# One slot's filler exchanged: Bm's products behind the gate's in slot 4, two blocks of y in slot 6, and the gate evicted at the end of slot 4

## What is computed

```
for each of the 128 steps:
    r        = decay * r + ctx_t * ctx_t
    inp      = (norm(x)_t * r) @ Wi.T + bi
    gate     = sigmoid(inp @ Wg.T + bg)
    blended  = gate * state + (1 - gate) * inp
    state    = tanh(blended @ A.T + inp @ Bm.T)
    out_t    = state @ Wo.T + bo
x = x + tanh(g_xattn) * out
x = x + tanh(g_ffn) * (relu(norm(x) @ Wq1.T + b1) @ Wq2.T + b2)
```

## Time and profile before

| | us |
|---|---|
| three timed executions | 319.73, 320.89, 321.32 (median 320.89) |
| the profiled execution | 319.58 |
| span of its instructions | 317.4 |
| PE busy (x3818) | 304.0 |
| PE weight loads busy | 278.1 |
| DVE busy (x816) | 283.4 |
| ACT busy (x556) | 236.9 |
| POOL busy (x138) | 78.5 |

### The profile page before, as it was taken

The page is one execution under the profiler, slowest core; times in us unless marked ns, Lnnn a source line. Parts: engine busy times, 40 slices in busy tenths (PEclk is TensorE's granted clock), DMA queues, the critical chain, the costliest instruction groups (busy, mean ns, idle before and its releaser), DMA issues. The chain is left out here.

```text
span 317.4 us, 10191 instructions
## 1 busy us (share of the span) xinstructions
PE 304.0 (96%) x3818; PEld 278.1 (88%) x3818; DVE 283.4 (89%) x816; ACT 236.9 (75%) x556; POOL 78.5 (25%) x138
## 2 busy tenths in 40 slices
PE   7889979999999999999999999999999999999995
PEld 5767868899999999999999999999999999997784
DVE  5889899999999999999999999999999998968763
ACT  4585548787778787887877787878877777857693
POOL 2021133241231323141412313231414121141230
PEclk9999999999999999999999999999999999999999
DMA  7903405123444435251533434441514314171321
GB/s 283 404 11 101 100 35 82 58 49 50 134 69 136 66 118 84 71 113 33 134 45 132 66 132 66 127 71 59 126 32 135 45 66 66 69 101 36 68 33 66
DMA packets 19399, 29.16 MB, mean 92 GB/s; under 512 B 1840, under 2 KB 10288, under 8 KB 19120
## 3 DMA queue, kind: packets, MB, share of 16 engines
q0 software_dynamic: 8720, 8.39, 18.5%
q1 hardware_dynamic: 10224, 19.93, 17.9%
q10 hardware_dynamic: 432, 0.53, 0.5%
HBM read 16.26 MB, written 4.19 MB: 64 GB/s over the span
## 5 line engine op out<-in xcount | busy, mean ns | idle before, releaser
L467 ACT ACTIVATE state<-pre_ps,sc 128x64 f32<-128x64 f32 x128 | 40.0, 312 | 51.2 <-PE pre_ps L1077 51.0
L457 ACT ACTIVATE hid<-hid_ps,b_s 128x256 f32<-128x256 f32 x120 | 50.2, 470 | 11.4 <-PE hid_ps L1116 9.7
L1116 PE MATMUL hid_ps<-xt_lo,w_q 128*128 128x256 f16 x240 | 55.5, 272 | 0.0
L1128 PE MATMUL y_ps<-w_q,h_lo 128*128 128x256 bf16 x240 | 55.5, 272 | 0.0
L1116 PE MATMUL hid_ps<-xt_hi,w_q 128*128 128x256 f16 x240 | 55.5, 272 | 0.0
L1128 PE MATMUL y_ps<-w_q,h_hi 128*128 128x256 bf16 x240 | 55.5, 272 | 0.0
L1071 PE MATMUL pre_ps<-m_hi,a_hi 128*128 128x32 f16 x508 | 42.6, 179 | 4.5 <-DVE m_hi L681 4.3
L732 DVE TENSOR_TENSOR h_lo<-hid,h_hi 128x512 f16<-128x512 f32 x60 | 41.3, 688 | 3.1 <-ACT h_hi L463 1.4
L1071 PEld LDWEIGHTS pre_ps<-m_hi,a_hi 128*128 128x128 f16 x508 | 33.7, 96 | 10.7 <-DVE m_hi L681 6.5
L1071 PE MATMUL pre_ps<-m_hi,a_lo 128*128 128x32 f16 x508 | 41.5, 177 | 0.0
L463 ACT CAST h_hi<-hid 128x512 f16<-128x512 f32 x60 | 37.1, 619 | 1.9
(11 more groups left out here) (181 smaller groups left out, 916.5 us busy)
## 6 DMA issues: line engine op xcount, KB each, us to landing
x_norm<-x_in SPq DMA_DIRECT2D x16, 256.0 KB, 2.7
cx<-ctx_in SPq DMA_DIRECT2D x16, 256.0 KB, 3.1
x_res<-x_in SPq DMA_DIRECT2D x16, 256.0 KB, 3.3
x_res<-bo_g POOLq DMA_DIRECT2D x16, 256.0 KB, 4.8
x<-b_g POOLq DMA_DIRECT2D x15, 256.0 KB, 3.9
y_out<-y SPq DMA_DIRECT2D x15, 256.0 KB, 2.0
w_raw<-w_in SPq DMA_DIRECT2D x2, 1024.0 KB, 8.4
wsq<-wsq_in SPq DMA_DIRECT2D x3, 256.0 KB, 5.1
```

Of the source, the lines that this page charges most:

```text
L457: last = nc.scalar.activation(hid[:, p % 2, u, :], hid_ps[p % 2][:, u * N:(u + 1) * N], ACT.Relu, bias=b1_s[:, 2 * p + u:2 * p + u + 1], s ...
L467: nc.scalar.activation(state[:, q[1] % 2, :, step_cols(j)], pre_ps[q[1] % 2][:, :].rearrange("p (k n) -> p k n", k=K)[:, :, step_cols(j)], ...
L1116: last = nc.tensor.matmul(hid_ps[p % 2][:, u * N:(u + 1) * N], w1_q[:, k, cut], v[:, par, k, :], start=n == 0, stop=n == len(terms) - 1)
L1128: last = nc.tensor.matmul(y_ps[:, t * D:(t + 1) * D], h[:, f, t * P:(t + 1) * P], w2_q[:, f, :], start=f == 0 and t == 0 and h is h_hi, st ...
```

## The change

Three pieces move, each within its engine's program. On PE the two `from_inp` calls go from slot 6 to slot 4, directly behind `gate_product`. Blocks 2 and 3 of y go from slot 4 to slot 6, ahead of blocks 6 and 7. On ACT `gate_out` goes from the start of slot 5's pieces (behind tanh 5) to the end of slot 4 (ahead of tanh 5). No instruction is added or removed, and DVE's, POOL's and SP's programs stay as they are.

```diff
@@ scalar engine, body
                     if j == 3 and project:
                         inp_out(project)
+                    if j == 4 and project:
+                        gate_out(project)
                     if j == 5:
-                        if project:
-                            gate_out(project)
                         if norm:
                             carry(project)
                             square(norm)
@@ tensor engine, body
                     if j == 2 and project:
                         inp_product(project)
-                    if j == 4 and ffn:
-                        if peeled == 2:
-                            pe.wait_ge(dve_prep, done[f"ternary{QUARTERS + 1}"])
-                        y_product(ffn, 2)
-                        y_product(ffn, 3)
                     if j == 4 and project:
                         gate_product(project)
+                        from_inp(project, 0)
+                        from_inp(project, 1)
                     if ffn:
-                        for f in {3: (0, 1), 5: (4, 5), 6: (6, 7)}.get(j, ()):
+                        for f in {3: (0, 1), 5: (4, 5), 6: (2, 3, 6, 7)}.get(j, ()):
@@
                     if project:
-                        if j == 6:
-                            from_inp(project, 0)
-                            from_inp(project, 1)
                         if j == 7:
                             from_rest(project)
```

## The result

The change makes the kernel slower: 324.59 us (median of six executions, 324.10 to 326.59) against 320.44 (six, 319.57 to 321.32), a ratio of 1.0143 with a 95% interval of 1.0116 to 1.0170 (the two medians alone give 1.0130). That is +4.15 us where +4.4 were forecast. The forecast of the time was 325.1, and 324.59 lies inside its range of 322.0 to 327.2. The profiled execution took 326.59 with a span of 323.3. It is the longest of the six. Its time lies 3.3 us above its span, where the other five lie 2.1 to 2.2 above theirs.

A forecast was written before the change was run, and what follows sets the result against it. PE and DVE were both taken to be at their limit, locking at step 4. Twelve intervals 3.0, iteration 1 1.1 and iteration 15 0.3 made +4.4 us; 320.89 + 4.4 = 325.3, forecast 325.1, range 322.0 to 327.2.

The forecast's parts named there:

- The ring: Step 4's low products to the next iteration's, through PE, ACT and DVE: +0.62 less 0.31, so 17.40 becomes 17.71 us.
- The term: Twelve intervals between step 4's low products, iteration 2 to 14: 3.0 us added, bounds 0 and 8.5.
- PE at step 7: Slot 6 shortens by about slot 4's gain, but PE waits at step 7 for m_lo 7, 0.31 later.
- PE's slot 4 and DVE's slot 6: Low products to step 5: 3.03 instead of 2.41 us; m_hi 6 to m_hi 7: 2.42 instead of 2.73, two waits gone.
- Iteration 1: No y blocks: slot 4 gains Bm's 1.41, DVE gives back 0.31, so +1.1 us, bounds 0 and 1.41.
- Iteration 15: Y blocks lengthen slot 6 by 0.79; 0.48 of waiting absorbs part, so +0.3 us passes on.
- The sum: Whole kernel: 3.0 + 1.1 + 0.3 = +4.4 us, span 317.4 + 4.4 = 321.8.
- Only the edges pay: Rival: DVE's gaps are room, intervals stay at 17.44, only iterations 1 and 15 cost; 322.3 us, chance 0.14.
- Slower still: Rival: slot 6's two DVE waits remain, each interval takes the whole 0.62; 329.6 us, chance 0.08.
- Faster: Rival: m_hi 6 doesn't inherit the later tanh 5, PE alone binds; 319.2 us, chance 0.06.
- the bracket at m_hi 6: Trace note on DVE ahead of m_hi 6: idle 0.22 us, released by tanh 5; cited against the faster rival.
- The rule of the Trainium skill: Optimize the highest-occupancy engine, TensorE judged by weight loads: names DVE, 89% against 88%; leads to the edges rival.

The follow-up runs named there:

- bm_only: Kernel before the change with only Bm's two calls moved behind the gate's product in PE's slot 4: 339.34 us against 319.66, ratio 1.0598.
- gate_out_late: Changed kernel with gate_out put back in slot 5, behind tanh 5: 328.45 us, ratio 1.0274 to the kernel without the change.
- gate_out_only: Kernel before the change with only gate_out moved ahead of tanh 5 on ACT: 321.86 us, ratio 1.0053.
- full_iterations_only: Changed kernel with the old PE order kept in iterations 1 and 15: 323.04 us, ratio 1.0088 to the kernel without the change.
- edges_only: Kernel before the change with the change made in iterations 1 and 15 alone: 321.60 us, ratio 1.0049.
- before_scan_early: Kernel before the change with DVE's scan moved to the end of slot 5, carry and square to ACT's slot 4: 328.16 us, ratio 1.0261.
- y_only: Kernel before the change with only y's blocks 2 and 3 moved from slot 4 to slot 6: 323.36 us, ratio 1.0110.
- scan_early: Changed kernel with DVE's scan at the end of slot 5, carry and square ahead of gate_out in ACT's slot 4: 322.50 us, ratio 1.0076 to unchanged.
- scan_early_full_only: Changed kernel with the scan moved early and the old PE order in iterations 1 and 15: 321.22 us, ratio 1.0035 to the kernel without the change.
- after: The kernel with the full change, against the kernel without it: 324.59 us, ratio 1.0143.
- before: The kernel without the change, the reference for the ratios: 320.44 us, median of six executions.

## Why the prediction was right

*The ring.* The two traces agree with it, and so do the intervals of bm_only, gate_out_late, gate_out_only, full_iterations_only, edges_only and before_scan_early: step 5 comes later by what PE's slot 4 holds more, and DVE has no room until the next step 4. y_only, scan_early and scan_early_full_only missed. The term was 3.0 and measured 2.84. Of it, scan_early shows 1.76 to be DVE's lane. The other 1.08 would be there without it, and are nearly all PE's own longer pass through slots 4 and 6. The prediction had this wrong: it took slot 6 to be shorter by what slot 4 is longer, or counted a gain of 0.08 per iteration. In after PE reaches step 7 6.70 behind step 4's low products (163.54 - 156.84), before 6.62. DVE's lane is longer still, 3.03 + 0.50 + 0.35 + 2.41 + 11.36 + 0.06 = 17.71 by the same sum as in the prediction, so the mistake had no effect on the forecast. It did on scan_early's.

*PE at step 7.* The prediction let PE wait there for DVE's 0.31. It waits for 0.03. The low products are wanted only 0.21 behind the start of the step, and before they started 0.25 behind the end of m_lo 7 (159.74 against 159.49), where a waiting PE starts 0.06 behind it. So the step had 0.19 of room, and 0.08 more came with PE's own delay. The reading of the earlier trace rows as the place where PE stops was wrong; the ring closes at the next step 4, through DVE's full lane, and the sum took it there.

*PE's slot 4 and DVE's slot 6.* 3.03 and 2.42 were forecast, 3.03 and 2.41 measured. The wait for the gate was the reason for the one gap and the square for the other: gate_out_late brings both back.

*Iteration 1.* The profiled execution alone would mislead: low products of step 4 in iterations 1 and 2 are 21.04 apart instead of 18.37. PE, start of step 4's low products, two of Bm's products, and step 5:

```profile
47.40 0.27 PE L1077 MATMUL pre_ps<-m_lo,a_hi 128*128 128x32 f16 x4
...
50.05 0.41 PE L1006 MATMUL pre_ps<-inp_lo,bm_hi 128*128 128x256 f32 x1
...
51.59 0.28 PE L1006 MATMUL pre_ps<-inp_hi,bm_hi 128*128 128x256 f32 x1
...
52.40 0.18 PE L1071 MATMUL pre_ps<-m_hi,a_hi 128*128 128x32 f16 x1
```

```profile
48.40:51.40 3.00, 3.00 (x16) 3.00 (x16) 1.54 (x5) 1.32 (x3) 1.51 (x2) 0.50 0.00 0
```

In the window the granted clock is 0.50, the 1.2 GHz level, and a matmul takes 0.41 instead of 0.28. From 47.40 to step 5 there are 5.00 us; at full clock scan_early has 3.47 for the same instructions. So 1.53 of the 2.67 are the clock, and 1.14 are left, for a forecast of 1.1. m_hi 6 to m_hi 7 there:

```profile
53.24 0.23 DVE L681 SCALAR_TENSOR_TENSOR m_hi<-state,gate 128x64 f16<-128x64 f32 x1 [3.26 <-ACT state L467]
55.64 0.20 DVE L681 SCALAR_TENSOR_TENSOR m_hi<-state,gate 128x64 f16<-128x64 f32 x1
```

2.40 instead of 2.73. That iteration 1 at full clock adds this much is also what edges_only leaves: its 1.5 less the 0.28 that its trace has behind iteration 15's step 4 are 1.2.

*Iteration 15.* Forecast 0.3. PE there, beside the earlier trace rows:

```profile
303.80 0.27 PE L1116 MATMUL hid_ps<-xt_hi,w_q 128*128 128x256 f16 x1
...
305.54 0.27 PE L1142 MATMUL att_ps<-wo_hi,s_hi 128*128 128x256 f16 x1
```

The sixteen matmuls take 1.74 and the wait for s_lo is gone. From iteration 15's step 4 (297.35) to the second row it is 8.19; before, 299.61 - 291.72 = 7.89. The difference is 0.30. That the forecast has the same number is partly luck: 1.74 was the middle between two paces, and y's pace of 0.79 for eight holds only ahead of a float32 product.

*The sum.* In spans it is 0.05 ahead of iteration 1, 2.67 there, 2.84, 0.07 from iteration 14 to 15, and 0.28 behind that: 5.9, of which 1.53 are the clock. Without it the span grows by 4.4, as forecast, and executions of after at full clock have 321.9 to 322.1 against a forecast of 321.8. That the sum meets 4.4 so closely is in part chance: the intervals gave 0.16 less, and small terms that the prediction didn't have (0.05 and 0.07, and 0.04 in iteration 1) gave it back. So is the 4.15 of the medians, since each of them mixes executions with and without the slow stretch; the spans at full clock are the better measure. The 325.1 started from 320.89, the median of three executions of before, where six have 320.44.

*The rivals.* "Only the edges pay" falls by edges_only (+1.5 us of 4.4) and by bm_only. "Slower still" is what gate_out_late does: 328.45 for a forecast of 329.6. "Faster" falls by the bracket at m_hi 6. The rule of the Trainium skill (Perfetto Trace Analysis, Identifying the Most-Contended Engine) doesn't lead to the answer here. Before, occupancy and weight loads name DVE (89% against 88%), whose lane is indeed one of the two limits, but that doesn't say what an exchange on PE costs. After the change they name PE (weight loads 88%, DVE 87%), and DVE's lane sets the interval. The same section also wants TensorE judged by the FLOPs it achieves, which the profile doesn't list.

What stays open is why every second interval in before is longer by 0.10, and what makes the clock fall. The first wasn't tried by itself. The trace shows where it lies: in iteration 8 tanh 1 starts 0.60 behind step 1 and m_hi 1 to m_hi 2 takes 2.21, in iteration 7 0.51 and 2.13, and PE waits for m_lo 4 in iteration 8. The prediction let this go with a later DVE; in after 0.05 or so of it are left, and in scan_early 0.13.

## What to carry to other kernels

Where several engines are near full, look for the ring that closes from one iteration to the next, and read each engine's waits along it. An exchange on one engine that leaves its instructions the same still moves its results in time, and costs what the fullest lane behind them can't absorb. It can also change the engine's own pace, by what now stands behind what (about 0.08 us in each interval here). A filler ahead of a step has a right length: too long delays the chain, and too short leaves the other engines no time for their own work. The same edit can gain or lose by several us depending on the slot's length, so edits on such a ring are to be weighed together.

## What the runs showed of the hardware

PE's granted clock fell to the 1.2 GHz level for 3.4 us in some executions and not in others of the same kernel, at a cost of about 1.5 us in the profiled execution of after. There it came in iteration 1; in the 7.9 us ahead of it PE was busy for 6.3:

```profile
39.50:47.40 7.90, 6.30 (x82) 4.84 (x80) 7.70 (x27) 3.66 (x9) 2.28 (x6) 1.00 0.14 39
```

That doesn't tell the two kinds of execution apart: in the profiles of before and scan_early, which have no slow stretch in iteration 1, PE was busy for 6.30 and 6.34 us in the same window.

With dummy matmuls in those waits the same part had PE busy for 7.42 of 7.50 us, and in that execution the stretch lay elsewhere:

```profile
40.50:48.00 7.50, 7.42 (x91) 5.96 (x90) 7.29 (x26) 3.38 (x9) 2.00 (x6) 1.00 0.11 39
```

A profile of one kind compared with the other kind is off by more than a third of this change.

What stands ahead of a float32 product decides whether its slow start costs anything: nothing measurable behind 16-bit products of 256 columns, about 0.08 us behind a step's low products of 32 columns (scan_early above).
